# Attention over 16 positions on Trainium2: the averages of one feature summed by TensorE instead of VectorE

## The chip, the cores and the metric

One core of one Trainium2 chip runs the whole program in one launch. The metric is the device time of an execution in microseconds (us). Shown are the median of several runs and one profiled execution with its own time.

## The reference, cut to what matters

The program is a model of four blocks, each with a cross attention, an attention and a feed-forward layer, on `x` of 64 x 32 x 128 (float32). The change lies in the attention layer of the last block:

```
def _L3_attn_ref(x, w_qkvw, w_out):
    H, G, DIM = 16, 4, 128
    HD = DIM // H // G                       # 2
    B, S, dim = x.shape
    qkvw = x @ w_qkvw
    chunks = jnp.split(qkvw, G, axis=-1)
    subs = [jnp.split(t, G, axis=-1) for t in chunks]
    q, k, v, w = (jnp.concatenate([subs[i][r] for i in range(4)], axis=0) for r in range(4))
    def shp(t):
        return t.reshape(B * G, H, -1, HD).swapaxes(1, 2)
    q, k, v = (shp(q), shp(k), shp(v))
    w = w.reshape(B * G, H, -1, HD)
    attn = jax.nn.softmax(q @ k.swapaxes(-2, -1) * HD ** (-0.5), axis=-1)
    o = (attn @ v).swapaxes(1, 2).reshape(B, S, dim)
    return o * w.reshape(B, S, dim) @ w_out
```

So there are 8192 small attentions. Each is over 16 positions, and each position has two features only.

## The kernel before, in words

The program is written by hand for each engine: every layer has a method for TensorE (`pe`), VectorE (`dve`), ScalarE (`act`), GpSimd (`pool`) and the DMA queue (`sp`). Each method issues its instructions in the order in which it is written, and semaphores order them against other engines (`done` names an event, `due` gives the waits for events). No scheduler moves anything.

The layer is `L3Attn`. A partition holds one of 128 groups. The features `z` (16 positions of 512) are cut into four chunks c of 128 features, and a chunk into two units, so there are eight units u. A unit is, for each partition, 8 attentions of 16 x 16 scores, 2048 numbers, or four banks of PSUM. Even units use banks 0 to 3, odd ones banks 4 to 7; `feature(u, r, f)` is feature f (0 or 1) of the queries, keys, values or gates (r = 0 to 3).

For a unit the steps are:

- **products** of queries and keys: of the first feature on GpSimd (L3514), of the second on VectorE (L3540);
- **add_products**: TensorE adds the two in PSUM by products of the identity, eight of 512 columns (L3454, L3455);
- **maxima**: VectorE takes the largest score of each row, with its sign turned (L3547);
- **subtract**: TensorE adds that to the scores, four products of the identity of 512 columns (L3464);
- **exponential**: ScalarE writes it to SBUF (L3499), and once more over the scores in PSUM (L3501);
- **weighing**: GpSimd multiplies the exponentials in SBUF by the values' first feature (L3524), VectorE those in PSUM by the second (L3561), after it has summed them (L3555) and taken the reciprocal (L3558). Both write to `vp`, one half each;
- **mix**: VectorE sums both halves of `vp` over the 16 positions (L3570, 4096 elements to 256), scales them by the reciprocals (L3574), and multiplies them by the gates (L3580, twice).

VectorE's order in the loop over u is mix(u-1), products(u+2), weigh(u), maxima(u+1). TensorE's is subtract(u), add_products(u+1), and at the end, for each chunk c, four transposes (L3478) and four products with `w_out` (L3484), between which ScalarE copies (L3506) and after which VectorE adds (L3599). The blocks of chunks 0 to 2 need mix(6), since they use its banks; that of chunk 3 needs mix(7) and its way through DRAM and back (L3428, L3432).

Of the kernel before, what the change touches and what calls it, by code (L numbers as in the profile page):

```python
# [10 lines left out]
ALU = mybir.AluOpType  # L11
ACT = mybir.ActivationFunctionType
AXX = mybir.AxisListType.X

P = 128
# [28 lines left out]
class Tally:  # L44
# [8 lines left out]
    def sem(self, name):  # L53
# [15 lines left out]
        "z": "lin_out", "z_out": "lin_out", "rows": "rows_out", "ffn_hidden": "lin_out", "products": "lin_out",  # L69
        "query_out": "lin_out", "located": "lin_out", "select": "cleared",  # L70
        "shifted": "beta", "list": "picked", "count": "picked", "end": "picked", "tiles": "picked", "past": "picked", "final": "residual", "exp_again": "exp",
        "weights6": "rows0", "weights7": "rows1", "tile8": "v30", "tile9": "v31", "tile10": "v32", "tile11": "v33"}
KIND.update({f"tile{k}": f"context{k}" for k in range(8)})

# [104 lines left out]
def spread(ap, shape, *axes):  # L179
    for ax in axes:  # L180
        ap = ap.unsqueeze(ax)
    return ap.broadcast_to(shape)


def quarter(ap, q):
    return ap[:, 4 * q:4 * q + 4, :]


def four(ap):
    return ap.rearrange("p (a d) -> p a d", a=4)  # L190
# [152 lines left out]
def cols(tag, q):  # L343

    return ("cols_dve" if q % 2 else "cols_act"), (tag, q)
# [419 lines left out]
class L0Cross(Layer):  # L765
    n, STEPS = 0, NT + 9
# [145 lines left out]
class L0Attn(Layer):  # L912
# [4 lines left out]
    n, SN, E, F, RING = 1, 16, 4, 256, 8  # L917
# [900 lines left out]
class L0Ffn(Layer):  # L1818
# [3 lines left out]
    n, E, unread = 2, 4, 8  # L1822
# [190 lines left out]
class L1Cross(Layer):  # L2013


    n, STEPS = 3, NT + 4
# [78 lines left out]
class L2Cross(Layer):  # L2095


    n, STEPS, unread = 6, NT + 6, 3
# [168 lines left out]
class L1Attn(Layer):  # L2267
# [3 lines left out]
    n = 4  # L2271
# [124 lines left out]
class L1Ffn(Layer):  # L2396


    n, E, HS = 5, 8, 512
# [128 lines left out]
class L2Attn(Layer):  # L2528
# [3 lines left out]
    n = 7  # L2532
# [96 lines left out]
class L2Ffn(Layer):  # L2629
# [3 lines left out]
    n, E, F = 8, 16, 512  # L2633
# [229 lines left out]
class L3Cross(Layer):  # L2863
# [7 lines left out]
    n, NH, DH, UL, NS = 9, 16, 64, U + S, 4  # L2871
# [513 lines left out]
class L3Attn(Layer):  # L3385
# [3 lines left out]
    n, NP, J, CN = 10, 16, 16, 4  # L3389
# [45 lines left out]
    def pe(self, e, T):  # L3435
        g, W, PS, NP, free = self.g, self.g.W, self.g.PS, self.NP, dict.fromkeys(range(8))
        self.start_pe(e, T, free)
        for c in range(self.CN):
            for k in range(4):
                b = 4 * ((c + 1) % 2) + k  # L3440
                for w in T.due(free[b], cols(10, 2), cols(10, 3)):
                    e.wait_ge(*w)
                for j in range(4):
                    h = 4 * k + j
                    m = e.matmul(PS[:, b, P * j:P * j + P], g.XT[:, P * h:P * h + P], W["a3_w"][:, P * c:P * c + P],
                                 start=True, stop=True)
                m.then_inc(*T.done("m3_z_out", (c, k)))
                free[b] = ("m3_z_act" if c or k % 2 == 0 else "m3_z_dve"), (c, k)

        def add_products(u):  # L3450
            for n, b in enumerate(self.banks(u)):
                for w in T.due(free[b], ("m3_first", u), ("m3_second_dve", u)):
                    e.wait_ge(*w)
                e.matmul(PS[:, b, :], g.C["ident"], self.pa[u % 2][:, 2 * n:2 * n + 2, :], start=True, stop=False)  # L3454
                m = e.matmul(PS[:, b, :], g.C["ident"], self.pb[u % 2][:, 2 * n:2 * n + 2, :], start=False, stop=True)  # L3455
            m.then_inc(*T.done("m3_scores", u))

        def subtract(u):
            w_ = 2 * NP
            for n, b in enumerate(self.banks(u)):  # L3460
                x = spread(self.least[:, u % 2, w_ * n:w_ * n + w_], [P, w_, NP], 2)
                for w in T.due(("m3_least", u)):
                    e.wait_ge(*w)
                m = e.matmul(PS[:, b, :].rearrange("p (r g) -> p r g", g=NP), g.C["ident"], x, start=False, stop=True,  # L3464
                             skip_group_check=True)
                free[b] = ("m3_mixed", u)
            m.then_inc(*T.done("m3_less", u))

        add_products(0)
        for u in range(self.NU):  # L3470
            subtract(u)
            if u + 1 < self.NU:
                add_products(u + 1)
        for c in range(self.CN):
            for w in T.due(free[c], (f"m3_back{c}", 0)):
                e.wait_ge(*w)
            for j in range(4):
                m = e.transpose(PS[:, c, P * j:P * j + P], self.back[c][:, j, :], g.C["ident"])  # L3478
            m.then_inc(*T.done("m3_back_turned", c))
            for w in T.due(("m3_backT", c)):  # L3480
                e.wait_ge(*w)
            for j in range(4):
                at = QW * c + P * j
                m = e.matmul(PS[:, c, P * j:P * j + P], g.XT[:, at:at + P], W["a3_wo"], start=True, stop=True)  # L3484
            m.then_inc(*T.done("m3_rows", c))
# [43 lines left out]
    def dve(self, e, T):  # L3529
        g, W, PS, NP, JU = self.g, self.g.W, self.g.PS, self.NP, self.JU  # L3530
        self.start_dve(e, T, by_position=True)
        for k in (1, 3):
            for w in T.due(("m3_z_out", (0, k))):
                e.wait_ge(*w)
            e.tensor_copy(self.z[:, 4 * k:4 * k + 4, 0:P], four(PS[:, 4 + k, :])).then_inc(*T.done("m3_z_dve", (0, k)))

        def products(u):
            for w in T.due(*self.features_in(u), ("m3_scores", u - 2)):
                e.wait_ge(*w)
            e.tensor_tensor(self.by_four(self.pb[u % 2]), spread(self.feature(u, 0, 1), self.wide, 3),  # L3540
                            spread(self.feature(u, 1, 1), self.wide, 2), ALU.mult).then_inc(*T.done("m3_second_dve", u))

        def maxima(u):
            rows = PS[:, 4 * (u % 2):4 * (u % 2) + 4, :].rearrange("p b (r g) -> p (b r) g", g=NP)
            for w in T.due(("m3_scores", u), ("m3_less", u - 2)):
                e.wait_ge(*w)
            e.tensor_reduce(self.least[:, u % 2], rows, AXX, ALU.max, negate=True).then_inc(*T.done("m3_least", u))  # L3547

        def weigh(u):

            k = u % 2
            total = self.total[:, k]
            for w in T.due(("m3_exp", u)):
                e.wait_ge(*w)
            e.tensor_reduce(total, self.ex[k].rearrange("p j (h g) -> p (j h) g", h=NP), AXX, ALU.add).then_inc(*T.step())  # L3555
            for w in T.due(T.prev()):
                e.wait_ge(*w)
            e.reciprocal(total, total).then_inc(*T.step())  # L3558
            for w in T.due(("m3_exp_again", u)):
                e.wait_ge(*w)  # L3560
            e.tensor_tensor(self.by_four(self.vp[k][:, 1].rearrange("p (j n) -> p j n", j=JU)), self.by_four(self.scores(u)),  # L3561
                            spread(self.feature(u, 2, 1), self.wide, 2), ALU.mult).then_inc(*T.step())

        def mix(u):

            k = u % 2
            total, mixed = self.total[:, k], PS[:, 4 * k, 0:2 * JU * NP]
            for w in T.due(("m3_weighed", u), T.prev()):
                e.wait_ge(*w)
            e.tensor_reduce(mixed, self.vp[k].rearrange("p e (r g) -> p (e r) g", g=NP), AXX, ALU.add).then_inc(*T.step())  # L3570
            mixed = mixed.rearrange("p (e r) -> p e r", e=2)
            for w in T.due(T.prev()):
                e.wait_ge(*w)
            e.tensor_tensor(mixed, mixed, spread(total, [P, 2, JU * NP], 1), ALU.mult).then_inc(*T.step())  # L3574
            for w in T.due(T.prev()):
                e.wait_ge(*w)
            n = D // 4 // 2
            dst = self.o[:, u // 2, :, n * (u % 2):n * (u % 2) + n].rearrange("p h (j e) -> p e j h", e=2)
            for f in range(2):
                m = e.tensor_tensor(dst[:, f], mixed[:, f].rearrange("p (j h) -> p j h", h=NP), self.feature(u, 3, f), ALU.mult)  # L3580
            m.then_inc(*T.done("m3_mixed", u))

        products(0)
        products(1)
        maxima(0)
        for u in range(self.NU):
            if u:
                mix(u - 1)
            if u + 2 < self.NU:
                products(u + 2)  # L3590
            weigh(u)
            if u + 1 < self.NU:
                maxima(u + 1)
        mix(self.NU - 1)
        for c in range(self.CN):
            x = quarter(g.X, c)
            for w in T.due(("m3_rows", c)):
                e.wait_ge(*w)
            e.tensor_tensor(x, four(PS[:, c, :]), x, ALU.add)  # L3599


class L3Ffn(Layer):
# [5 lines left out]
    n, ends, E, F, K = 11, 12, 8, 512, 2  # L3608
# [671 lines left out]
```

## Time and profile before

| | us |
|---|---|
| median of 3 runs | 2239.46 (2231.65 to 2241.68) |
| profiled execution | 2235.21 |
| its span | 2233.1 |
| granted clock of TensorE, mean over the span | 0.913 |

The span is the time between the first and the last instruction of the profiled execution; its own time has what lies around it as well. The layer `L3Attn` lies between about 1803 and 1978 us of that span. In the rows below PE is TensorE (PEld its weight load), DVE VectorE, ACT ScalarE, POOL GpSimd and SPq the DMA queue of SyncE. A float32 product is recorded as two MATMUL records, so four products of the program are x8. The granted clock is given as a share: 1.00 is 2.4 GHz and 0.50 is 1.2 GHz.

### The profile page before, as it was taken

The page shows a single profiled execution, that of the slowest core. Times are in us where ns is not written, and L with a number is a line of the kernel's source. Part 1 is how long each engine was busy: PE and PEld are TensorE (multiplying, and loading weights), DVE is VectorE, ACT ScalarE, POOL GpSimd, SP SyncE. Part 2 cuts the span into 40 slices and gives each one's busy share as a digit, 9 for nine tenths or more (in the row PEclk, how much of TensorE's full clock was granted, in tenths as well). Part 3 has the DMA queues.
Part 4 walks back from the last instruction along what each step waited for, and adds up shares of the span by engine and source line. Part 5 has one row for each costly group of instructions (what it writes and reads, how often), then busy time and mean ns, then how long its engine had stood idle before and what let it go on. Part 6 is the DMA issues. An engine that isn't in the chain of part 4 may idle for free. (4 is left out here: it accounts for less than half of the span.)

```text
span 2233.1 us, 50173 instructions
## 1 busy us (share of the span) xinstructions
PE 1875.5 (84%) x20208; PEld 1205.0 (54%) x20208; DVE 1517.1 (68%) x3652; ACT 971.5 (44%) x2471; POOL 731.1 (33%) x955
## 2 busy tenths in 40 slices
PE   6768999899889799996677699999999987757396
PEld 3324557555554556543557566666666652335286
DVE  4799995788865765547861577666666479977722
ACT  2445664566633722232412355555655421216143
POOL 2244554455530614204340401000000056434443
PEclk9779999999999999998779999999999998868588
DMA  9000000100035000160034101000000000012087
GB/s 372 36 1 0 1 1 1 72 5 4 5 155 198 33 1 1 48 274 1 2 117 143 45 20 39 12 18 20 20 12 9 1 1 10 19 63 105 27 280 243
DMA packets 56086, 134.79 MB, mean 60 GB/s; under 512 B 13913, under 2 KB 34092, under 8 KB 48176
## 3 DMA queue, kind: packets, MB, share of 16 engines
q1 hardware_dynamic: 52560, 125.48, 15.8%
q0 software_dynamic: 3296, 6.12, 0.8%
q8 instruction: 160, 2.62, 0.5%
q14 instruction: 70, 0.57, 0.1%
HBM read 112.13 MB, written 20.12 MB: 59 GB/s over the span
## 5 line engine op out<-in xcount | busy, mean ns | idle before, releaser
L317 POOL TENSOR_TENSOR arena<-arena 128x4 f32<-128x4 f32 (+2 forms) x101 | 115.5, 1145 | 843.1 <-DVE arena L261 405.5
L3219 ACT ACTIVATE arena<-PS,arena 128x289 f32<-128x289 f32 x256 | 126.8, 505 | 178.3 <-DVE arena L3324 178.3
L364 PE MATMUL PS<-arena 128*128 128x512 f32 x286 | 159.0, 674 | 5.0 <-DVEq L4081 4.2
L1799 POOL TENSOR_TENSOR arena<-arena 128x128 f32<-128x128 f32 x384 | 140.2, 403 | 50.7 <-PE PS L1662 27.8
L3107 PE MATMUL PS<-arena 128*128 128x289 f32 x512 | 135.5, 408 | 2.3 <-DVE arena L3318 1.8
L1735 DVE RECIPROCAL arena<-PS 128x128 f32<-128x128 f32 x96 | 91.7, 955 | 52.7 <-PE PS L1700 52.6
L1766 ACT COPY arena<-PS 32x128 f32<-32x128 f32 x384 | 99.3, 259 | 50.7 <-PE PS L1676 46.2
L1185 POOL TENSOR_TENSOR arena<-arena 128x512 f32<-128x512 f32 x64 | 85.0, 1328 | 108.9 <-DVE arena L1330 108.9
L384 PE MATMUL PS<-arena 128*128 128x128 f32 x288 | 51.1, 318 | 68.7 <-DVE arena L296 30.4
L3107 PEld LDWEIGHTS PS<-arena 128*128 128x128 f32 x512 | 92.2, 190 | 24.2 <-issue 2.6
L3324 DVE TENSOR_REDUCE arena<-PS 128x2 f32<-128x578 f32 x128 | 92.6, 754 | 7.2 <-PE PS L3107 6.0
L403 ACT COPY arena<-PS 128x512 f32<-128x512 f32 x40 | 24.4, 610 | 166.1 <-PE PS L384 165.9
L456 PE MATMUL PS<-arena 128*128 128x128 f32 (+4 forms) x576 | 85.2, 294 | 12.9 <-DVE arena L411 4.1
L456 PEld LDWEIGHTS PS<-arena 128*128 128x128 f32 (+1 forms) x576 | 78.5, 214 | 26.3 <-issue 7.7
L2444 PE MATMUL PS<-arena 128*128 128x512 f32 x192 | 90.7, 607 | 0.0
L3121 PE MATMUL PS<-arena 128*128 128x128 f32 x512 | 78.5, 283 | 12.9 <-DVE arena L3337 11.7
L420 PE MATMUL PS<-arena 128*128 128x512 f32 x160 | 81.7, 631 | 7.1 <-DVE arena L411 3.2
L384 PEld LDWEIGHTS PS<-arena 128*128 128x128 f32 x288 | 37.9, 162 | 91.3 <-issue 41.6
L3337 DVE TENSOR_SCALAR arena<-arena 128x290 f32<-128x290 f32 x256 | 84.0, 371 | 4.6
L1325 DVE TENSOR_TENSOR_SCAN arena<-arena 128x512 f32<-128x512 f32 x64 | 85.4, 1335 | 0.0
L364 PEld LDWEIGHTS PS<-arena 128*128 128x128 f32 x286 | 54.0, 213 | 52.6 <-issue 50.5
L3097 PE MATMUL PS<-arena 128*128 128x128 f32 x512 | 69.1, 284 | 13.8 <-ACT arena L3236 7.1
(411 smaller groups left out, 4779.4 us busy)
## 6 DMA issues: line engine op xcount, KB each, us to landing
arena<-in_ctx SPq DMA_DIRECT2D x48, 1090.0 KB, 7.0
arena<-in_f_w SPq DMA_DIRECT2D x39, 514.0 KB, 4.9
lists<-arena SPq DMA_DIRECT2D x8, 1040.0 KB, 10.9
arena<-in_f_w SPq DMA_DIRECT2D x32, 256.0 KB, 2.9
arena<-in_ctx SPq DMA_DIRECT2D x16, 512.0 KB, 4.0
arena<-in_mid SPq DMA_DIRECT2D x1, 3796.5 KB, 11.9
arena<-in_late SPq DMA_DIRECT2D x1, 3204.0 KB, 11.5
arena<-in_w SPq DMA_DIRECT2D x1, 3017.0 KB, 13.3
```

The costliest lines, as they stand in the source:

```text
L317: e.tensor_tensor(x, x, half.broadcast_to(list(x.shape)), ALU.pow).then_inc(*T.done("norm_root", tag))
L364: e.matmul(g.PS[:, b, :], g.C["ident"], g.const_words[:, 0:512], start=True, stop=True)
L384: i = e.transpose(g.PS[:, b, P * j:P * j + P], src[:, 4 * q + j, :], g.C["ident"])
L456: i = e.matmul(g.PS[:, b, n * j:n * j + n], src[:, at:at + P], w_, start=True, stop=True)
L1325: e.tensor_tensor_scan(self.Ur[:, j % R, :], self.Ar[:, j % R, :], self.Ur[:, j % R, :], 0.0, ALU.mult, ALU.add).then_inc(*T.done("a0_scan ...
L1735: e.reciprocal(rest, PS[:, 7, P:2 * P]).then_inc(*T.step())
L1766: k = e.copy(v[r, :, h, :], PS[r, 4, 0:P].rearrange("p (a d) -> p a d", d=HD))
L1799: k = e.tensor_tensor(dst[:, b], spread(src[:, b, :], [P, HG, S], 1), spread(self.g.C["headmask"], [P, HG, S], 2), ALU.mult)
L2444: e.matmul(g.PS[:, b, :], w_, g.XT[:, cut(q)], start=True, stop=True).then_inc(*T.done(name, k))
L3107: m = e.matmul(PS[:, k, 0:UL], self.qt[i % 2][:, j, P * k:P * k + P], self.kt[i % 3][:, j, :], start=True, stop=True)
L3219: e.activation(self.weights(n, k, 0, UL), PS[:, k, 0:UL], ACT.Exp, bias=self.st[:, h, k:k + 1], accum_out=self.st[:, h, 4 + k:5 + k]).then ...
L3324: e.tensor_reduce(self.st[:, n % 2, 2 * k:2 * k + 2], PS[:, 2 * k:2 * k + 2, 0:UL], AXX, ALU.max, negate=True).then_inc(*T.done("k3_least" ...
```

## The change

The first half of `vp` (the first feature's products) is no longer summed by VectorE. TensorE sums it: a new function `sums(u)` issues sixteen products of the identity, one for each position, all into the same 128 columns of the unit's second bank. The n-th reads every sixteenth element of `vp`'s first half, beginning with the n-th. It waits for both weighings of the unit. VectorE sums the other half alone, into the unit's first bank, and then waits for TensorE before it scales. The scaling becomes two instructions of 128 elements each.

```
--- before.py
+++ after.py
@@ -69,6 +69,7 @@
         "z": "lin_out", "z_out": "lin_out", "rows": "rows_out", "ffn_hidden": "lin_out", "products": "lin_out",
         "query_out": "lin_out", "located": "lin_out", "select": "cleared",
         "shifted": "beta", "list": "picked", "count": "picked", "end": "picked", "tiles": "picked", "past": "picked", "final": "residual", "exp_again": "exp",
+        "wide": "weighed",
         "weights6": "rows0", "weights7": "rows1", "tile8": "v30", "tile9": "v31", "tile10": "v32", "tile11": "v33"}
 KIND.update({f"tile{k}": f"context{k}" for k in range(8)})
 
@@ -3466,11 +3467,23 @@
                 free[b] = ("m3_mixed", u)
             m.then_inc(*T.done("m3_less", u))
 
+        def sums(u):
+
+            v0 = self.vp[u % 2][:, 0].rearrange("p (r g) -> p r g", g=NP)
+            for w in T.due(("m3_weighed", u), ("m3_wide", u)):
+                e.wait_ge(*w)
+            for n in range(NP):
+                m = e.matmul(PS[:, 4 * (u % 2) + 1, 0:self.JU * NP], g.C["ident"], v0[:, :, n], start=n == 0, stop=n == NP - 1)
+            m.then_inc(*T.done("m3_summed", u))
+
         add_products(0)
         for u in range(self.NU):
+            if u:
+                sums(u - 1)
             subtract(u)
             if u + 1 < self.NU:
                 add_products(u + 1)
+        sums(self.NU - 1)
         for c in range(self.CN):
             for w in T.due(free[c], (f"m3_back{c}", 0)):
                 e.wait_ge(*w)
@@ -3559,25 +3572,25 @@
             for w in T.due(("m3_exp_again", u)):
                 e.wait_ge(*w)
             e.tensor_tensor(self.by_four(self.vp[k][:, 1].rearrange("p (j n) -> p j n", j=JU)), self.by_four(self.scores(u)),
-                            spread(self.feature(u, 2, 1), self.wide, 2), ALU.mult).then_inc(*T.step())
+                            spread(self.feature(u, 2, 1), self.wide, 2), ALU.mult).then_inc(*T.done("m3_wide", u))
 
         def mix(u):
 
             k = u % 2
-            total, mixed = self.total[:, k], PS[:, 4 * k, 0:2 * JU * NP]
-            for w in T.due(("m3_weighed", u), T.prev()):
-                e.wait_ge(*w)
-            e.tensor_reduce(mixed, self.vp[k].rearrange("p e (r g) -> p (e r) g", g=NP), AXX, ALU.add).then_inc(*T.step())
-            mixed = mixed.rearrange("p (e r) -> p e r", e=2)
-            for w in T.due(T.prev()):
-                e.wait_ge(*w)
-            e.tensor_tensor(mixed, mixed, spread(total, [P, 2, JU * NP], 1), ALU.mult).then_inc(*T.step())
-            for w in T.due(T.prev()):
-                e.wait_ge(*w)
+            total, mixed = self.total[:, k], [PS[:, 4 * k + 1, 0:JU * NP], PS[:, 4 * k, 0:JU * NP]]
+            for w in T.due(("m3_wide", u)):
+                e.wait_ge(*w)
+            e.tensor_reduce(mixed[1], self.vp[k][:, 1].rearrange("p (r g) -> p r g", g=NP), AXX, ALU.add).then_inc(*T.step())
             n = D // 4 // 2
             dst = self.o[:, u // 2, :, n * (u % 2):n * (u % 2) + n].rearrange("p h (j e) -> p e j h", e=2)
             for f in range(2):
-                m = e.tensor_tensor(dst[:, f], mixed[:, f].rearrange("p (j h) -> p j h", h=NP), self.feature(u, 3, f), ALU.mult)
+                for w in T.due(*([T.prev()] if f else [("m3_summed", u)])):
+                    e.wait_ge(*w)
+                e.tensor_tensor(mixed[f], mixed[f], total, ALU.mult).then_inc(*T.step())
+            for f in range(2):
+                for w in T.due(T.prev()):
+                    e.wait_ge(*w)
+                m = e.tensor_tensor(dst[:, f], mixed[f].rearrange("p (j h) -> p j h", h=NP), self.feature(u, 3, f), ALU.mult)
             m.then_inc(*T.done("m3_mixed", u))
 
         products(0)
```

TensorE's order, around the subtraction of one unit. Before (L3464 is the subtraction, L3454 and L3455 the additions):

```order
L3455 MATMUL PS<-arena 128x512
L3464 MATMUL PS<-arena 128x512 x4
L3454 MATMUL PS<-arena 128x512
L3455 MATMUL PS<-arena 128x512
L3454 MATMUL PS<-arena 128x512
```

And now, where lines have moved by one (L3465 is the subtraction, L3455 and L3456 the additions, L3476 the new products):

```order
L3456 MATMUL PS<-arena 128x512
L3476 MATMUL PS<-arena 128x128 x16
L3465 MATMUL PS<-arena 128x512 x4
L3455 MATMUL PS<-arena 128x512
L3456 MATMUL PS<-arena 128x512
L3455 MATMUL PS<-arena 128x512
```

The sixteen products of the unit before stand ahead of the subtraction. At the end of the layer TensorE's order was (L3478 transposes of an output block, L3484 its products):

```order
L3464 MATMUL PS<-arena 128x512 x4
L3478 MATMUL PS<-arena 128x128 x4
L3484 MATMUL PS<-arena 128x128 x4
L3478 MATMUL PS<-arena 128x128 x4
L3484 MATMUL PS<-arena 128x128 x4
```

and it is now (L3491 and L3497 are those two lines):

```order
L3465 MATMUL PS<-arena 128x512 x4
L3476 MATMUL PS<-arena 128x128 x16
L3491 MATMUL PS<-arena 128x128 x4
L3497 MATMUL PS<-arena 128x128 x4
L3491 MATMUL PS<-arena 128x128 x4
```

The last unit's sums stand ahead of all four output blocks. VectorE's order in a unit, now (L3560 maxima, L3583 the halved sum, L3589 the two scalings, L3593 the gates, L3553 the products, L3568, L3571 and L3574 the weighing):

```order
L3560 TENSOR_REDUCE arena<-PS 128x128
L3583 TENSOR_REDUCE PS<-arena 128x128
L3589 TENSOR_TENSOR PS<-PS,arena 128x128 x2
L3593 TENSOR_TENSOR arena<-PS,arena 128x8x16 x2
L3553 TENSOR_TENSOR arena<-arena 128x2048
L3568 TENSOR_REDUCE arena<-arena 128x128
L3571 RECIPROCAL arena<-arena 128x128
L3574 TENSOR_TENSOR arena<-PS,arena 128x2048
```

Nothing has moved there but the scaling, which is two instructions where it was one.

## Rows read from the trace of the kernel before

**Rows 1.** The page: busy time by engine; the chain that ended last.
```profile
PE 1875.5 (84%) x20208; PEld 1205.0 (54%) x20208; DVE 1517.1 (68%) x3652; ACT 971.5 (44%) x2471; POOL 731.1 (33%) x955
...
PE PS L3107 3%; PE PS L3097 3%; PE PS L3155 3%; PE PS L3774 2%; PE PS L3783 2%; PE PS L3147 2%; PE PS L3139 2%; PE PS L3121 2%; PE PS L3140 2%; ACT arena L3219 1%; ACT arena L3211 1%; PE PS L2731 1%; DVE arena L3561 1%; DVE PS L3570 1%; DVE arena L3337 1%
```

**Rows 2.** Window: us, busy us (x instructions) of PE, PEld, DVE, ACT, POOL, PEclk.
```profile
1844.00:1862.00 18.00, 13.03 (x25) 5.42 (x24) 17.90 (x10) 3.65 (x2) 11.19 (x2) 0.78 0.00 0
```

**Rows 3.** Timeline, VectorE, one unit: start us, us, engine, line, shapes, count.
```profile
1839.23 2.29 DVE L3547 TENSOR_REDUCE arena<-PS 128x128 f32<-128x2048 f32 x1
1841.43 4.42 DVE L3570 TENSOR_REDUCE PS<-arena 128x256 f32<-128x4096 f32 x1
...
1845.89 0.43 DVE L3574 TENSOR_TENSOR PS<-PS,arena 128x256 f32<-128x256 f32 x1
...
1846.36 0.65 DVE L3580 TENSOR_TENSOR arena<-PS,arena 128x128 f32<-128x128 f32 x2
...
1846.92 3.71 DVE L3540 TENSOR_TENSOR arena<-arena 128x2048 f32<-128x2048 f32 x1
...
1850.55 2.28 DVE L3555 TENSOR_REDUCE arena<-arena 128x128 f32<-128x2048 f32 x1
...
1852.86 0.95 DVE L3558 RECIPROCAL arena<-arena 128x128 f32<-128x128 f32 x1
...
1853.73 3.54 DVE L3561 TENSOR_TENSOR arena<-PS,arena 128x2048 f32<-128x2048 f32 x1
...
1857.19 2.28 DVE L3547 TENSOR_REDUCE arena<-PS 128x128 f32<-128x2048 f32 x1
```

**Rows 4.** Timeline, the other engines; in brackets idle time before and what ended it.
```profile
1826.92 3.70 PE L3464 MATMUL PS<-arena 128*128 128x512 f32 x8 [2.38 <-DVE arena L3547]
...
1841.58 6.11 PE L3464 MATMUL PS<-arena 128*128 128x512 f32 x8 [4.09 <-DVE arena L3547]
...
1847.73 1.88 ACT L3499 ACTIVATE arena<-PS 128x2048 f32<-128x2048 f32 x1 [13.42 <-PE PS L3464]
...
1849.68 6.36 POOL L3524 TENSOR_TENSOR arena<-arena 128x2048 f32<-128x2048 f32 x1 [6.70 <-ACT arena L3499]
```

**Rows 5.** Timeline: products of 128 columns at either clock; groups: VectorE, L1738.
```profile
1803.14 5.04 PE L3445 MATMUL PS<-arena 128*128 128x128 f32 x43 [1.20 <-DVE arena L411]
...
1964.71 2.07 PE L3484 MATMUL PS<-arena 128*128 128x128 f32 x8 [0.67 <-ACT arena L3506]
...
L1738 DVE TENSOR_TENSOR arena<-PS,arena 128x128 f32<-128x128 f32 x96 | 28.1, 293 | 3.3
```

**Rows 6.** VectorE reading in order (L3599, groups) and with a stride (L3540, timeline).
```profile
L3599 DVE TENSOR_TENSOR arena<-PS,arena 128x512 f32<-128x512 f32 x4 | 2.6, 683 | 8.3 <-PE PS L3484 8.3
...
1826.79 3.62 DVE L3540 TENSOR_TENSOR arena<-arena 128x2048 f32<-128x2048 f32 x1
```

**Rows 7.** Busy time and granted clock (PEclk) in three windows.
```profile
1824.60:1826.90 2.30, 0.00 (x0) 0.00 (x0) 2.30 (x2) 0.00 (x0) 0.09 (x1) 1.00 0.00 0
1837.50:1841.50 4.00, 0.00 (x0) 0.00 (x0) 4.00 (x3) 0.00 (x0) 4.00 (x2) 0.77 0.00 0
...
1839.60:1846.50 6.90, 4.92 (x6) 2.19 (x7) 6.83 (x4) 0.00 (x0) 3.39 (x1) 0.51 0.00 0
```

**Rows 8.** Timeline, units 6 and 7: a wait of VectorE, and a subtraction.
```profile
1938.86 2.29 DVE L3555 TENSOR_REDUCE arena<-arena 128x128 f32<-128x2048 f32 x1 [2.15 <-ACT arena L3499]
...
1947.86 5.40 PE L3464 MATMUL PS<-arena 128*128 128x512 f32 x8 [3.96 <-DVE arena L3547]
```

**Rows 9.** Timeline, the end of the stage: output blocks, store and read.
```profile
1959.37 1.06 PE L3478 MATMUL PS<-arena 128*128 128x128 f32 x4
...
1962.97 1.06 PE L3478 MATMUL PS<-arena 128*128 128x128 f32 x4
...
1967.66 1.23 SPq L3428 DMA_DIRECT2D mixed<-arena  x2
...
1973.77 1.12 PE L3478 MATMUL PS<-arena 128*128 128x128 f32 x4 [6.99 <-DMA arena<-mixed]
```

## The prediction

> **What bounds the kernel now.** I read the page first. TensorE is busy for 84% of the span and VectorE for 68%, but the chain that ended last gives the lines of this layer 1% at most [rows 1]. That is an average over twelve layers, so the worth of the change has to be read from its own stretch, about 1803 to 1978 us. The busy times there turn the picture over: in an 18 us window VectorE works 17.90 us and TensorE 13.03 [rows 2]. VectorE is the bound of the middle of this stage.
>
> The timeline of one unit says how [rows 3]. The maxima of one unit start at 1839.23 and those of the next at 1857.19, so a unit takes 17.96 us, and VectorE has no idle time in brackets inside it. Its largest items are the sums over positions at L3570 (4.42 us), the products L3540 (3.71) and the weighing L3561 (3.54).
>
> The other engines fit inside that [rows 4]. TensorE waits 4.09 us for the maxima and subtracts them in 6.11 us. The same subtraction took 3.70 us at 1826.92, where the clock was full. ScalarE's exponential takes 1.88 us and GpSimd's weighing 6.36. None of them is waited for by VectorE in this unit: 6.11 instead of 3.70 costs nothing today.
>
> **The change, part by part.** VectorE. L3570 sums 4096 elements, and will sum 2048. The row of L3555, a sum of 2048 contiguous elements, gives 2.28 us [rows 3], so 2.14 go. The scaling L3574 (0.43 us for 256 elements) becomes two of 128. The nearest row of that shape is 0.293 us [rows 5], so 0.16 come, and 0.04 for one more hand-over, the gap between L3570's end and L3574's start being that small. VectorE's unit falls by 1.94 us to 16.0.
>
> TensorE. It gains sixteen products of the identity with 128 columns. Each is two records, as for every float32 product here, so 32 records. At the full clock 43 records of 128 columns took 5.04 us [rows 5]: without the tail of the last, 0.113 each, so 3.6 us for the sixteen products. At half the clock eight took 2.07 us with their tail, so about 7.4 for 32 and 8.3 at most. These products lie on a new path. They start when VectorE and GpSimd have both weighed unit u-1, and the subtraction for unit u is queued behind them on TensorE. The path around, from one weighing's end to the next, is then: hand-over 0.1, sums 3.6, subtraction with its tail 3.75, exponential 1.88, hand-over 0.1, total 2.31, reciprocal 0.87, weighing 3.54 [rows 3 to 5]. That is 16.15 us, as long as VectorE's own 16.0. So at the full clock a unit takes about 16.15 us, 1.8 less than now, and VectorE is relieved just to the point where the new path takes over. GpSimd's weighing ends 6.36 us after its start, VectorE's 6.7 after the exponential: GpSimd sets nothing as long as it is not slowed by more than 0.4.
>
> The clock. TensorE now stands still for 4 us and more in a unit, the granted clock falls in that pause (0.77 over it), and it stays at 1.2 GHz for the next 7 us (0.51) [rows 7]. A pause of 2.3 us left it at 2.4 GHz (1.00). After the change TensorE works 3.6 + 3.4 + 6.9 = 13.9 us of 16.15 (the additions are eight products against the subtraction's four), which leaves a pause of 2.2 us. That is nearest to the row that kept its clock, but a little overlap with slower work makes it longer, so I choose: it falls in three of five units. What a fall costs is bounded by the subtractions: 6.11 against 3.70 is 2.4 us, and 5.40 [rows 8] against 3.70 is 1.7. TensorE will now resume sooner after it stopped, so I take 1.7. What was hidden lies on the path now. A unit with a fall takes 17.85 us and gains 0.1.
>
> The sum. Five intervals (units 1 to 5) have the full VectorE load: two gain 1.8, three gain 0.1, together -3.9 us. In units 6 and 7 VectorE has no products left and already waits for the exponential, 2.15 us [rows 8]. There the path is the bound today: maxima 2.28, hand-over 0.1 and subtraction 5.40, 7.8 us. It becomes 0.1 + 3.6 + 3.7 + 1.7 = 9.1: +1.3 twice, +2.6. After the last weighing VectorE needs 4.42 + 0.47 + 0.65 = 5.5 us today. Then it will wait for sixteen products on a TensorE that has stood still for some 8 us. These take between 3.6 and 7.4, taken as 5 since the clock comes back on the way, then 0.3 + 0.65 + 0.65, that is 6.6 to 7.0 or up to 9.0: +1.5 taken, +3.5 at worst. Last, the output blocks of chunks 0 to 2 stand behind these sums in TensorE's order, where they ran beside VectorE's last unit. A block takes 3.60 us at the half clock (1959.37 to 1962.97) [rows 9], so 10.8 for three. Chunk 3's store and read cover 6.1 us (1967.66 to 1973.77) plus 1.6 of scaling before. At the full clock the blocks fit, at the half clock they are 3.1 too long. I take nothing, since the sums have just woken the clock. In all -3.9 + 2.6 + 1.5 = +0.2 us. Against the profiled execution (span 2233.1, 2235.21 us with what lies around it) that is 2235.4. The median of the runs is 2239.46, 0.2% above it, and the forecast on it is 2239.5 (2239.46 + 0.2, rounded). Measurement tells about 0.5%, 11.2 us, from nothing.
>
> **The unknown price.** No row shows TensorE reading its moving operand with a stride, and the new products take every sixteenth element. The ends: nothing (0.113 us a record, as contiguous), or what VectorE shows. Its contiguous 512 elements took 0.683 us, and 2048 of L3540, whose inner elements lie 2 KB apart, 3.62 [rows 6]: 1.33 and 1.77 ns an element with the fixed part, and 1.12 against 1.77 if the sum L3555 is the measure. At 1.77 ns a record would need 0.227 us and the sixteen products 7.2. TensorE's record takes 0.88 ns a column for its own work already, and part of a slower read would vanish behind that, so I take nothing and keep 7.2 for the range. The Trainium skill (SBUF — State Buffer, Door 1, the note on cachelines) says that reads stay at full rate only if at least two fall in a 16-byte line; here each falls in its own. By that rule the sums would be the slow end, and the time the second rival's. The VectorE rows agree with it; no row shows it of TensorE.
>
> **The rivals.** (1) *The clock stays up.* Every pause is 2.2 us, like the one of 2.3 that kept it. Five units gain 1.8, units 6 and 7 gain 0.4 each (7.4 against 7.8), the tail still costs 1.2: -8.6, 2230.9 us. For it: that row. Against: the pauses are as near to it as 0.1 us, so any that is longer counts, and the row with 4.0 fell. (2) *The strided products are slow, and the kernel is slower.* At 7.2 us for the sums the path is 19.75 us, 1.8 over today, in five units: +9.0. In units 6 and 7 it is 11.0 against 7.8: +6.4. The tail is 7.2 + 1.6 against 5.5: +3.3. In all +18.7, 2258.2 us, with the clock up, since TensorE hardly pauses. It passes the 0.5% from about 0.39 us a product on. (3) *Between them*: 0.36 us a product by VectorE's ratio of 1.6 puts 2.2 us on the path: 0.4 x 5 + 1.8 x 2 + 1.9 = +7.5, 2247.0 us. (4) *It does not do what it says.* If GpSimd's weighing is slowed beside L3540, it and not VectorE releases the sums. Half a microsecond a unit, +2.5: 2242. The order of the changed program shows the products where the diff puts them, so nothing else of this kind is open.
>
> **How the numbers follow.** Forecast with its clock falls 0.45, rival 1 0.14, rival 3 0.14, rival 4 0.03, rival 2 0.19, and 0.05 for a strided price above 7.2 us. The time is the forecast's, 2239.5. The low end is rival 1 with the runs' scatter of some 4 us, 2227. The high end takes in rival 2, 2258, and leaves out what is dearer. Faster by over 0.5%: only rival 1 with everything else right, 0.09. Slower: rival 2 and what is beyond, 0.25. Within: 0.66.
>
> **What would show it.** The reduction at 2.3 us. The maxima 16 to 18 us apart, by turns, instead of 17.96. Sums with records 0.113 us apart at the full clock; 0.2 or more there is rival 2. Brackets of idle time before the exponential's readers on VectorE, a fraction of a microsecond in the middle and near 4 us in units 6 and 7. Granted clock over the middle above 0.9. The forecast is wrong if the maxima are 19 us apart, or if all five intervals are 16.2.

## The result and the profile after

The changed kernel takes 2258.45 us (median of 10 runs, 2246.39 to 2270.25) against 2240.09 us (10 runs, 2231.65 to 2241.68) for the kernel before. The ratio is 1.0084, with a 95% interval of 1.0065 to 1.0103, so the change makes the kernel slower by 0.8%. The profiled execution took 2264.29 us with a span of 2262.2 us and a mean granted clock of 0.921.

The page's line of busy times, of the changed kernel:

```profile
PE 1906.2 (84%) x20464; PEld 1245.4 (55%) x20464; DVE 1496.2 (66%) x3660; ACT 971.0 (43%) x2471; POOL 725.9 (32%) x955
```

TensorE has gained 30.7 us of busy time and VectorE has lost 20.9, where [rows 1] had 1875.5 and 1517.1.

The timeline of one middle unit, all engines but the weight loads, answers to [rows 3, 4]:

```profile
1863.99 2.27 DVE L3560 TENSOR_REDUCE arena<-PS 128x128 f32<-128x2048 f32 x1
...
1864.21 7.19 PE L3476 MATMUL PS<-arena 128*128 128x128 f32 x32 [1.99 <-DVE arena L3574]
1866.20 2.27 DVE L3583 TENSOR_REDUCE PS<-arena 128x128 f32<-128x2048 f32 x1
...
1871.23 3.61 PE L3465 MATMUL PS<-arena 128*128 128x512 f32 x8
1871.44 0.63 DVE L3589 TENSOR_TENSOR PS<-PS,arena 128x128 f32<-128x128 f32 x2 [2.98 <-PE PS L3476]
...
1872.11 0.65 DVE L3593 TENSOR_TENSOR arena<-PS,arena 128x128 f32<-128x128 f32 x2
...
1872.67 3.66 DVE L3553 TENSOR_TENSOR arena<-arena 128x2048 f32<-128x2048 f32 x1
...
1874.88 1.88 ACT L3512 ACTIVATE arena<-PS 128x2048 f32<-128x2048 f32 x1 [15.83 <-PE PS L3465]
...
1876.79 2.29 DVE L3568 TENSOR_REDUCE arena<-arena 128x128 f32<-128x2048 f32 x1 [0.46 <-ACT arena L3512]
...
1876.83 5.54 POOL L3537 TENSOR_TENSOR arena<-arena 128x2048 f32<-128x2048 f32 x1 [9.10 <-ACT arena L3512]
...
1879.11 0.95 DVE L3571 RECIPROCAL arena<-arena 128x128 f32<-128x128 f32 x1
...
1879.98 3.57 DVE L3574 TENSOR_TENSOR arena<-PS,arena 128x2048 f32<-128x2048 f32 x1
...
1883.46 2.29 DVE L3560 TENSOR_REDUCE arena<-PS 128x128 f32<-128x2048 f32 x1
```

L3560 is the maxima, L3583 the halved sum, L3589 the two scalings, L3593 the gates, L3553 the products, L3568, L3571 and L3574 the weighing. On the other engines L3476 is the new products, L3465 the subtraction, L3512 the exponential and L3537 GpSimd's weighing. The maxima start at 1863.99 and at 1883.46: a unit takes 19.47 us where it took 17.96. The sum is halved as planned (2.27 us). But TensorE's 32 new records take 7.19 us, the subtraction is queued behind them and begins at 1871.23, and VectorE waits for them before it scales, 2.98 us, and again for the exponential, 0.46 us. The path of the prediction is all there, in order: VectorE's weighing of the unit before, the sums, the subtraction, the exponential, and the weighing of this unit.

Busy time in two windows of 18 us in the middle of the stage, which answer to [rows 2], and in one of 3.4 us at the start of the last unit's sums:

```profile
1864.00:1882.00 18.00, 17.50 (x56) 11.26 (x56) 14.46 (x11) 3.65 (x2) 8.90 (x2) 0.91 0.14 31
1903.00:1921.00 18.00, 17.50 (x56) 11.07 (x56) 14.45 (x11) 3.65 (x2) 8.89 (x2) 1.00 0.14 31
1981.00:1984.40 3.40, 3.37 (x15) 3.40 (x16) 2.22 (x1) 0.00 (x0) 0.00 (x0) 0.50 0.00 0
```

TensorE is now busy for 17.50 us of 18 and VectorE for 14.46. They have changed places. The window at 1981 shows 15 records of the sums in 3.4 us at the half clock. In the window at 1903 the clock is full, and that unit's sums took as long as any other's (7.20 us).

Who waited for whom between 1840 and 1960 us (engine and line, the one waited for, us in total, times, longest):

```profile
DVE PS L3589 <- PE PS L3476: 17.9, 6, 3.0
...
DVE arena L3568 <- ACT arena L3512: 8.5, 7, 4.0
```

VectorE waits for the new products in every unit.

By parts of the stage, between the profile shown of before and this one: the five full units take 97.4 us instead of 89.7 (+7.7), unit 6 takes 19.47 instead of 16.58 (+2.9), the way from the last maxima to the next layer 37.8 instead of 33.0 (+4.8), and the way to the first maxima 25.8 instead of 21.4 (+4.3). The last is of another kind: in this execution VectorE had both its first products done before GpSimd had its first, whose record is 12.1 us long instead of 8.5, and the additions started later, at the half clock. None of the eight profiles of the experiments shows it (21.4 us in each). Together the stage takes 195.1 us instead of 175.4, +19.7. The spans of the two profiles are 29.1 us apart. Most of the rest lies in the last layer, which took 168.5 us here and 159.4 in the profile shown of before; the kernel before, run once more below, bears on that.

### The profile page after: what moved, and what is told of

Its sections match the earlier page's. It is cut to its first block, busy times and chain, and to the rows that moved or that the text cites. A ratio compares the mean times of both kernels' runs of the same rounds, so it can differ in the third digit from the quotient of the medians.

```text
span 2262.2 us, 50693 instructions
## 1 busy us (share of the span) xinstructions
PE 1906.2 (84%) x20464; PEld 1245.4 (55%) x20464; DVE 1496.2 (66%) x3660; ACT 971.0 (43%) x2471; POOL 725.9 (32%) x955
## 3 DMA queue, kind: packets, MB, share of 16 engines
q0 software_dynamic: 3296, 6.12, 0.8%
## 4 chain that ended last, share of the span: by engine, by line
PE 54%; DVE 26%; issue 8%; ACT 8%; POOL 1%; DMA 1%; SPq 1%; POOLq 0%; another core or an unknown queue 0%; DVEq 0%; ACTq 0%
PE PS L2445 3%; PE PS L421 3%; PE PS L3108 3%; PE PS L457 3%; PE PS L3098 3%; PE PS L3476 3%; PE PS L3156 3%; PE PS L365 3%; DVE arena L1736 2%; PE PS L2245 2%; DVE arena L251 2%; PE PS L3787 2%; PE PS L3796 2%; PE PS L3148 2%; PE PS L3140 1%
## 5 line engine op out<-in xcount | busy, mean ns | idle before, releaser
L365 PE MATMUL PS<-arena 128*128 128x512 f32 x286 | 154.0, 655 | 5.0 <-DVEq L4094 4.2
L3108 PEld LDWEIGHTS PS<-arena 128*128 128x128 f32 x512 | 92.2, 190 | 24.2 <-issue 2.9
L385 PEld LDWEIGHTS PS<-arena 128*128 128x128 f32 x288 | 37.2, 161 | 98.1 <-issue 43.0
L2445 PE MATMUL PS<-arena 128*128 128x512 f32 x192 | 91.2, 610 | 0.0
L421 PE MATMUL PS<-arena 128*128 128x512 f32 x160 | 81.4, 629 | 7.3 <-DVE arena L412 3.8
L3122 PEld LDWEIGHTS PS<-arena 128*128 128x128 f32 x512 | 60.6, 142 | 36.4 <-issue 17.7
```

The source lines that it names most:

```text
L365: e.matmul(g.PS[:, b, :], g.C["ident"], g.const_words[:, 0:512], start=True, stop=True)
L421: e.matmul(g.PS[0:w_.shape[-1], b, :], w_, src[:, cut(q)], start=True, stop=True).then_inc(*T.done("lin_out", (tag, q)))
L2445: e.matmul(g.PS[:, b, :], w_, g.XT[:, cut(q)], start=True, stop=True).then_inc(*T.done(name, k))
L3108: m = e.matmul(PS[:, k, 0:UL], self.qt[i % 2][:, j, P * k:P * k + P], self.kt[i % 3][:, j, :], start=True, stop=True)
L3122: m = e.transpose(PS[:, b, P * k:P * k + P], self.weights(n, k, at, at + P), g.C["ident"])
```

## The experiments

All are compared with the kernel before on the same chip (medians 2243.64 us of 25 runs in the first set of four, 2243.34 of 17 in the second). The diffs are against the changed kernel, unless another is named.

### Reading in order

```
-            v0 = self.vp[u % 2][:, 0].rearrange("p (r g) -> p r g", g=NP)
+            v0 = self.vp[u % 2][:, 0].rearrange("p (n r) -> p r n", n=NP)
```

> Each of the sixteen products reads 128 neighbouring elements instead of every sixteenth; nothing else changes. (The averages of the first feature are then sums of other elements.) Theory A, the strided read is what makes the sums slow: their records stand 0.113 us apart at the full clock instead of 0.222, 32 of them take 3.6 to 4.9 us instead of 7.2, the maxima of the middle units stand 16 to 17.7 us apart instead of 19.5, and the kernel takes 2232 to 2243 us. Rival B, TensorE is slowed by something else in these products (VectorE's maxima beside them, or adding sixteen times to the same columns): the records stay 0.22 us apart and the time stays at 2258. Rival C, the time is lost in the wait order and not in the products: records at 0.113, but the time above 2250.

It took 2239.47 us, ratio 0.9975 (0.9956 to 0.9994). The sums in two units, from TensorE's timeline, and the granted clock over each, from the windows:

```profile
1854.54 5.44 PE L3476 MATMUL PS<-arena 128*128 128x128 f32 x32 [1.96 <-DVE arena L3574]
...
1872.25 3.81 PE L3476 MATMUL PS<-arena 128*128 128x128 f32 x32 [1.97 <-DVE arena L3574]
```

```profile
1854.50:1859.70 5.20, 5.16 (x31) 5.19 (x32) 4.30 (x2) 0.00 (x0) 3.59 (x1) 0.67 0.01 3
1872.20:1875.80 3.60, 3.55 (x32) 3.58 (x33) 3.60 (x2) 0.00 (x0) 3.60 (x1) 1.00 0.00 0
```

32 records take 3.81 us at the full clock, against 7.19 to 7.20 with every sixteenth element in the middle units; with a fall of the clock they take 5.44, more than the 4.9 expected at most. By their starts in the trace the records stand 0.112 us apart at the full clock and 0.213 at the half one. With the stride it is 0.218 at either clock. The unit in whose sums the clock had fallen takes 17.71 us and the next 16.08. Theory A holds. Rivals B and C fall: nothing but the order of reading was changed. With it the units became 3.4 us shorter where the clock stayed up and 1.8 where it fell. Each against the kernel before of its own set of runs, the two kernels are 22.5 us apart (+18.36 and -4.17).

### Written by position, read in order

```
-            v0 = self.vp[u % 2][:, 0].rearrange("p (r g) -> p r g", g=NP)
+            v0 = self.vp[u % 2][:, 0].rearrange("p (n r) -> p r n", n=NP)
...
-            v2 = self.vp[k].rearrange("p e (j h g) -> p e j h g", j=self.JU, h=self.NP)
+            v2 = self.vp[k].rearrange("p e (g j h) -> p e j h g", j=self.JU, h=self.NP)
```

> The whole computation is kept: GpSimd writes the weighed first feature position by position, with its inner step 512 bytes, so that TensorE can read in order. Theory A: TensorE as with reading in order, 2232 to 2243 us, if GpSimd's weighing stays at 5.5 us. If a strided write costs GpSimd what strided reads seem to cost (5.5 to 8 us), its weighing ends after VectorE's and up to 2 us a unit come on top: up to 2255. Rival B: 2258 or more.

It took 2238.69 us, ratio 0.9980 (0.9958 to 1.0003). GpSimd's weighing, with a step of 512 bytes between the elements it writes (durations in ns: least, median, most):

```profile
L3537 POOL TENSOR_TENSOR arena<-arena x8: 5554/5580/5597, 1832.6 to 1951.7; 128x2048 f32<-128x2048 f32 x8
```

That is what it took with neighbouring elements (5.54 us in the unit above). A strided write costs GpSimd nothing here, so the whole computation can be had with TensorE reading in order. The units are those of the kernel that reads in order to 0.1 us. The interval of the ratio takes in 1: this kernel can't be told from the kernel before the change.

### A ladder of steps

```
-            v0 = self.vp[u % 2][:, 0].rearrange("p (r g) -> p r g", g=NP)
+            v0 = self.vp[u % 2][:, 0].rearrange("p (r g) -> p r g", g=(1, 2, 3, 4, 5, 8, 16, 16)[u]) if u not in (2, 4) else \
+                self.vp[u % 2][:, 0, 0:(3 * 682 if u == 2 else 5 * 409)].rearrange("p (r g) -> p r g", g=(3 if u == 2 else 5))
...
-                m = e.matmul(PS[:, 4 * (u % 2) + 1, 0:self.JU * NP], g.C["ident"], v0[:, :, n], start=n == 0, stop=n == NP - 1)
+                m = e.matmul(PS[:, 4 * (u % 2) + 1, 0:self.JU * NP], g.C["ident"],
+                             v0[:, 0:self.JU * NP, n % (1, 2, 3, 4, 5, 8, 16, 16)[u]], start=n == 0, stop=n == NP - 1)
```

> The products of unit 0 to 7 read their elements with a step of 1, 2, 3, 4, 5, 8, 16 and 16 elements. (The averages of the first feature are then sums of other elements.) Theory A with the 16-byte lines of the Trainium skill: 0.113 us a record at the full clock for steps 1 and 2, where two reads fall in a line, and 0.222 from step 4 on; step 3 between. Rival: the price grows smoothly with the step, and 16 is dearer than 8. At the half clock all are near 0.22.

One run, 2258.15 us. The sums of units 0 to 6, steps 1, 2, 3, 4, 5, 8 and 16, in TensorE's timeline:

```profile
1839.64 3.81 PE L3476 MATMUL PS<-arena 128*128 128x128 f32 x32 [1.99 <-DVE arena L3574]
...
1855.75 5.47 PE L3476 MATMUL PS<-arena 128*128 128x128 f32 x32 [1.99 <-DVE arena L3574]
...
1873.48 5.70 PE L3476 MATMUL PS<-arena 128*128 128x128 f32 x32 [1.97 <-DVE arena L3574]
...
1891.48 7.47 PE L3476 MATMUL PS<-arena 128*128 128x128 f32 x32 [1.99 <-DVE arena L3574]
...
1911.23 7.60 PE L3476 MATMUL PS<-arena 128*128 128x128 f32 x32 [1.99 <-DVE arena L3574]
...
1931.13 7.69 PE L3476 MATMUL PS<-arena 128*128 128x128 f32 x32 [1.99 <-DVE arena L3574]
...
1951.09 7.20 PE L3476 MATMUL PS<-arena 128*128 128x128 f32 x32 [1.97 <-DVE arena L3574]
```

And the granted clock over the sums with steps 1, 2, 3 and 5:

```profile
1839.80:1843.40 3.60, 3.60 (x33) 3.60 (x33) 3.60 (x2) 0.00 (x0) 3.39 (x1) 1.00 0.00 0
1855.80:1861.20 5.40, 5.40 (x33) 5.40 (x34) 4.20 (x2) 0.00 (x0) 3.48 (x1) 0.68 0.01 3
1873.50:1879.10 5.60, 5.60 (x33) 5.60 (x34) 4.24 (x2) 0.00 (x0) 3.55 (x1) 1.00 0.00 0
1911.30:1918.80 7.50, 7.50 (x33) 6.79 (x34) 4.19 (x2) 0.00 (x0) 3.48 (x1) 1.00 0.00 0
```

Step 2 took 5.47 us with the clock at the half level for part of it, which is what step 1 took in the same case above (5.44). Step 3 took 5.70 at the full clock where step 1 took 3.81. From step 4 on it is 7.2 to 7.7. By the records' starts at the full clock: 0.112, 0.114, 0.170, 0.227, 0.230, 0.232 and 0.218 us for the seven steps. So neighbours and every second element cost the same, every third half as much again, and from 16 bytes on it is twice as much and nearly flat. The rival, a smooth growth, falls: step 16 is no dearer than step 8. This is what the Trainium skill says of cachelines (SBUF — State Buffer, Door 1): two reads in a line of 16 bytes keep the full rate. The trace agrees, with 0.114 us at 8 bytes and 0.227 at 16. The same note gives four float32 as what can be stridden for free; if that means a step of four, the measurement is against it. In time a column that has a line to itself takes 1.70 to 1.81 ns, close to the 1.77 of VectorE's strided product [rows 6].

### The sums left out

```
-            if u:
-                sums(u - 1)
             subtract(u)
...
-        sums(self.NU - 1)
...
-                for w in T.due(*([T.prev()] if f else [("m3_summed", u)])):
+                for w in T.due(*([T.prev()] if f else [("m3_weighed", u)])):
```

> TensorE's sums are left out, VectorE waits for GpSimd's weighing instead and sums the second feature only. (The averages of the first feature are left out.) This is the change with its new work free. Theory A: VectorE is the bound again with 16.0 us a unit, and 2 us fall away after the last unit: 2225 to 2230 us. If the clock's falls now show (subtraction 6 us instead of 3.7 in the path), units of 16.5 and 2232. Rival C, the waits are what costs: above 2240.

It took 2239.75 us, ratio 0.9979 (0.9963 to 0.9995). That is no faster than with the sums in order. Every middle unit takes 17.06 to 17.10 us. Two lines of the timeline, the subtraction on TensorE and the total on VectorE:

```profile
1860.52 6.12 PE L3465 MATMUL PS<-arena 128*128 128x512 f32 x8 [4.10 <-DVE arena L3557]
...
1868.59 2.29 DVE L3565 TENSOR_REDUCE arena<-arena 128x128 f32<-128x2048 f32 x1 [1.17 <-ACT arena L3509]
```

TensorE stands still for 4.10 us before the subtraction, which then takes 6.12 us, most of it at the half clock. Before the change this was hidden [rows 4]; with VectorE relieved of 2 us it is not, and VectorE waits 1.17 us for the exponential. The first expectation (16.0 us a unit, 2225 to 2230 us) was wrong. The second was right about the clock but not about its size (16.5 us a unit, 2232). The time is next to rival C's mark (above 2240), but the wait that shows is the one for the slow subtraction and the exponential behind it. The sums in order are nearly free: with them TensorE pauses for 2.0 us and not 4.1, and the subtraction took 3.6 us at the full clock in every unit. Five units take 85.3 us with them and 85.4 without.

### Half of the strided products

```
-            for n in range(NP):
+            for n in range(NP // 2):
```

> The change with eight strided products instead of sixteen. (Positions 8 to 15 are left out of the first feature's averages.) Theory A says only the products' time matters: 8 of 0.436 us are as long as 16 in order at the full clock, so 3.5 us of sums at either clock, the maxima of the middle units 16.0 to 16.2 us apart and the time like that of reading in order or 1 to 2 us under it, 2236 to 2240. If the stride also hurts something beside TensorE (VectorE or GpSimd reading the same memory), the units stay above 17 us and the time above 2245.

It took 2241.05 us, ratio 0.9983 (0.9967 to 0.9999), and the middle units 15.97, 16.24, 16.65, 16.85 and 16.94 us. TensorE's timeline in one of them, the eight products and the subtraction:

```profile
1877.03 3.70 PE L3476 MATMUL PS<-arena 128*128 128x128 f32 x16 [1.97 <-DVE arena L3574]
1880.55 4.27 PE L3465 MATMUL PS<-arena 128*128 128x512 f32 x8
```

The sums take 3.70 us, close to what sixteen in order take at the full clock (3.81). The expectation was missed in part: only the first unit is at 16.0 us, and the time is 1 us above the 2240 that was the upper end. What is above 16 us is the subtraction (4.27 instead of 3.6 here, 3.61 to 4.68 over the units), whose beginning runs at the half clock in every unit shown but the first. The stage is 169.8 us long. So the stride costs TensorE's own time and nothing is seen of it beside TensorE: VectorE's sum (2.28 us) and GpSimd's weighing (5.54) are as long as with reading in order.

### The kernel before, once more

> The kernel before once more, for its last layer: 159.4 us passed there from the layer's first product to its first expert product in the profile shown, and 168.6 to 174.2 in the five later kernels, none of which touches it. If that is the change's doing (where instructions lie, or the clock), this profile shows 159 again. If it is scatter of single executions, it shows up to 174 here.

One run, 2239.79 us. The first and last start of its first expert products (line, engine, count, durations in ns, starts in us):

```profile
L3774 PE MATMUL PS<-arena x312: 275/275/552, 2142.1 to 2215.7; 128*128 128x128 f32 x156
```

Its last layer begins at 1972.6 us, so 169.5 us pass there, 10 more than in the profile shown (159.4). The seven changed kernels have 167.5 to 174.2. So the 9 us between the two profiles above are no sign of a cost of the change: the kernel before has them too in this execution. With one more profile a smaller effect on the last layer isn't ruled out. The stage of this profile takes 176.6 us, 1.2 more than in the one shown, so a difference of that size in a single stage is scatter too.

### Two halves

Against the kernel that is written by position. In VectorE's weighing:

```
-            e.tensor_tensor(self.by_four(self.vp[k][:, 1].rearrange("p (j n) -> p j n", j=JU)), self.by_four(self.scores(u)),
-                            spread(self.feature(u, 2, 1), self.wide, 2), ALU.mult).then_inc(*T.done("m3_wide", u))
+            half = JU // 2
+            for x in (slice(0, half), slice(half, JU)):
+                out = self.by_four(self.vp[k][:, 1].rearrange("p (j n) -> p j n", j=JU)[:, x])
+                e.tensor_tensor(out, self.by_four(self.scores(u)[:, x]), spread(self.feature(u, 2, 1)[:, x], [P, half, NP, NP], 2),
+                                ALU.mult).then_inc(*(T.step() if x.start else T.done("m3_wide", u)))
...
-            for w in T.due(("m3_wide", u)):
+            for w in T.due(T.prev()):
                 e.wait_ge(*w)
             e.tensor_reduce(mixed[1], self.vp[k][:, 1].rearrange("p (r g) -> p r g", g=NP), AXX, ALU.add).then_inc(*T.step())
```

> The whole computation is kept. To the kernel that reads in order, VectorE's weighing is cut in two halves, and TensorE's sums wait for the first half alone, which frees the bank they write to. The path falls by 1.2 us, to where GpSimd's weighing (5.6 us after the exponential) sets it, and TensorE's pause falls from 2.0 us to 0.9. If pauses under 1 us keep the clock, all middle units take 16.1 to 16.2 us (VectorE's own work and 0.1 for the cut) instead of 16.1 and 17.7 by turns: 5 us less than reading in order alone, 2233. If the clock falls all the same: 2238.

It took 2229.29 us (6 runs), ratio 0.9932 (0.9909 to 0.9955): 0.7% faster than before the change, with the whole computation. The sums in a middle unit, and GpSimd's next weighing:

```profile
1859.36 3.84 PE L3476 MATMUL PS<-arena 128*128 128x128 f32 x32 [1.78 <-POOL arena L3537]
...
1868.63 6.66 POOL L3537 TENSOR_TENSOR arena<-arena 128x2048 f32<-128x2048 f32 x1 [4.46 <-ACT arena L3512]
```

A window of 16 us over one unit:

```profile
1859.00:1875.00 16.00, 14.14 (x56) 8.05 (x56) 15.90 (x12) 3.65 (x2) 11.54 (x3) 1.00 0.15 34
```

The sums now wait for GpSimd. Where its weighing overlaps VectorE's products it takes 6.6 to 6.7 us, and TensorE's pause before the sums is 1.77 to 1.84 us (four of seven); elsewhere the weighing takes 5.57 and the pause is 0.75 (three of seven). Expected was 0.9. The granted clock fell after one of the four longer pauses and after none of the short ones; in the next kernel below it fell after none of five of 1.75 to 1.84. Reading in order, it fell after four of seven pauses of 1.96 to 2.00 us. VectorE works 15.90 us of 16, so it is the bound again. The middle units take 16.0, 15.9, 16.0, 16.4 and 16.0 us. It is 9.4 us under the kernel written by position, and 10.2 under the one that only reads in order, where 5 were expected. The stage is 161.6 us long instead of 171.6: 5.0 of that in the five full units, 1.3 in unit 6, and 3.8 from the last maxima on.

### Two halves, and the last unit as before the change

Against the kernel with two halves; VectorE sums both features of the last unit, and GpSimd writes that unit's half in the old order.

```
-        sums(self.NU - 1)
...
+            last = u == self.NU - 1
...
+            if last:
+                for w in T.due(("m3_weighed", u)):
+                    e.wait_ge(*w)
+                e.tensor_reduce(mixed[0], self.vp[k][:, 0].rearrange("p (r g) -> p r g", g=NP), AXX, ALU.add).then_inc(*T.step())
...
-                for w in T.due(*([T.prev()] if f else [("m3_summed", u)])):
+                for w in T.due(*([T.prev()] if f or last else [("m3_summed", u)])):
```

> The whole computation is kept. As the kernel with the two halves, but the last unit's two sums are both VectorE's, as before the change, so that nothing waits for a TensorE that has stood still, and the output blocks are not held back. That saves 5.1 + 0.3 + 0.65 - 2.2 us less 0.4, near 1.5 us after the last unit: 2231.5, and about 0.4% under the kernel before. If the output blocks set the end in any case, nothing.

It took 2226.65 us (6 runs), ratio 0.9938 (0.9914 to 0.9962). Against 0.9932 that is no gain, and its stage is 162.5 us long where the last was 161.6. The end of the stage in this kernel and in the last one, from chunk 3's store to the next layer's first product:

```profile
1949.91 1.23 SPq L3429 DMA_DIRECT2D mixed<-arena  x2
...
1955.98 1.11 PE L3490 MATMUL PS<-arena 128*128 128x128 f32 x4 [8.39 <-DMA arena<-mixed]
...
1960.71 7.36 PE L365 MATMUL PS<-arena 128*128 128x512 f32 x12 [0.86 <-DVEq L4102]
```

```profile
1960.53 1.23 SPq L3429 DMA_DIRECT2D mixed<-arena  x2
...
1966.55 0.66 PE L3491 MATMUL PS<-arena 128*128 128x128 f32 x4 [0.60 <-DMA arena<-mixed]
...
1969.90 5.39 PE L365 MATMUL PS<-arena 128*128 128x512 f32 x12 [0.86 <-DVEq L4097]
```

VectorE saves nothing: the store begins 20.9 us after the last maxima (1929.03), where it began 20.8 after them (1939.69) with the sums on TensorE. There the sums had started 1.2 us before VectorE's own (1953.50 and 1954.71), and VectorE then waited 2.17 us for them, about as long as its second sum takes here (2.28). And the fourth output block, from its transposes to the next layer, takes 4.7 us at the half clock, where it took 3.4 at the full one behind the last sums.

## Why the prediction was wrong

The forecast was no change, 2239.5 us (2239.46 + 0.2 is 2239.7; the slip changes nothing), and the range ended at 2258. The measured 2258.45 lies at the second rival's 2258.2. That the two agree to 0.3 us is luck, as the parts below show.

**The step that failed** is the unknown price: "part of a slower read would vanish behind that, so I take nothing and keep 7.2 for the range". Nothing vanished. A product's record needs 0.218 us with the stride against 0.113 taken, and the sixteen products 7.19 us against the 3.6 of the sum. The other end of the range had 7.2. The rows pointed there: VectorE pays 1.77 ns for an element that lies in a line of its own, and TensorE's 0.88 ns a column is less than that. The end should have been chosen that is nearest to a strided row, not the one of a contiguous row. The price as read from VectorE, 0.227 us a record, was within 5%.

**The path** was right. Its members were named, and each is in the unit above. With 7.2 us for the sums it was to be 19.75 us; it is 19.46 to 19.50. Five units cost +7.7 against 9.0 worked out, unit 6 +2.9 against 3.2. From the last maxima on it is +4.8 against 6.5, and most of that difference is the fourth output block, which took 3.4 us at the full clock instead of 4.7 at the half one; no term of the prediction has it. That is +15.4 against the rival's +18.7. The profile's +19.7 has the +4.3 at the start as well, which the prediction did not have. How often that start occurs was not tried, so some 3 us of the 18.4 between the medians stay open.

**VectorE's part** was right: 2.27 us for the sum (2.28), 0.63 for the two scalings (0.59), 16.06 us for a unit without a fall of the clock (reading in order; 16.0 to 16.15).

**The clock.** "It falls in three of five units" and costs 1.7 was chosen between two rows. Reading in order shows 16.06, 17.71, 16.08, 17.71 and 17.75 us: three of five, and 1.65 us. The count was a choice, so its coming out is luck. With the stride the clock fell as well, in the sums behind five of the seven pauses of 1.96 to 1.99 us (0.76 over those sums), but it cost nothing there, since these run at 0.218 us a record at either clock, and by the subtraction it had come back (3.61 us at 1.00 in every unit). Rival 2's remark that TensorE hardly pauses was wrong: the pause is as long as in the forecast.

**The sum for the sums in order** was +0.2 us; its stage came out 3.8 us shorter than in the profile of before. The five units gave -4.4 against -3.9. Unit 6 was taken at +1.3 with a fall of the clock; its clock stayed up, and it gave -0.5. From the last maxima on it was +1.15 against 2.8. Of that, unit 7 (+1.25, taken at 1.3) and the way from the last weighing to the store (+1.26, taken at 1.5) came as worked out. The rest is the fourth output block, which TensorE ran at the full clock behind the sums: 3.35 us from its transposes to the next layer instead of 4.72. The prediction let the sums wake the clock for the first three blocks and left out the fourth.

**Rival 4** was wrong in the changed kernel (GpSimd's weighing took 5.54 us and set nothing), but GpSimd is what sets the start of the sums once VectorE's weighing is cut in two.

## What to carry to other kernels

Before work is moved to TensorE as products of the identity, look at the step between the elements of the moving operand. In float32 up to 8 bytes are free here, and 16 bytes or more double the product at the full clock; if another engine writes the operand, let that engine write it in the order in which TensorE will read it. A pause of TensorE that is hidden today is on the path as soon as the bound beside it is relieved, so that a small amount of work in the pause can cost nothing: here the sums in order took no more time than none at all. And work that is queued ahead of an instruction that others wait for is paid in full, so its wait should name the least that it needs.

## What was not expected of the hardware

- A strided product ignores the granted clock: 0.218 us a record of 128 columns at 1.2 and at 2.4 GHz, with the elements 64 bytes apart. In order it is 0.213 and 0.112.
- Step 16 (0.218) is a little cheaper than steps 5 and 8 (0.230 and 0.232). Why is open.
- GpSimd's product took 5.58 us writing with a step of 512 bytes, and 5.54 writing neighbours, with the same reads.
- At the start of the stage GpSimd's product is recorded with 8.5 us and VectorE's second with 8.5, where later ones take 4.9 and 3.7 alone. In the changed kernel's profile VectorE's two take 3.7 each and GpSimd's first 12.1. The lengths fit one of the two engines working at a time (3.7 + 4.9 and 3.7 + 3.7 + 4.9); no run tests it.
- The last layer of one and the same kernel took 159.4 and 169.5 us in two executions.
